# Six of the eight weight-chunk splits moved from setup to beside the first pair product

## The reference, cut to what matters

```python
def cell(h, x):
    gi = x @ W_ih + b_ih
    gh = h @ W_hh + b_hh
    i_r, i_z, i_n = jnp.split(gi, 3, axis=-1)
    h_r, h_z, h_n = jnp.split(gh, 3, axis=-1)
    r = jax.nn.sigmoid(i_r + h_r)
    z = jax.nn.sigmoid(i_z + h_z)
    n = jnp.tanh(i_n + r * h_n)
    h_new = (1.0 - z) * n + z * h
    return (h_new, h_new)
...
x = x + ffn(gru(cond_2048, x))
```

## Time and profile before

| | us |
|---|---|
| median of the runs | 2902.66 |
| the profiled execution's own time | 2908.95 |
| its span, first to last instruction | 2907.2 |
| setup, to the start of the next block | 139.26 |
| PE busy in the span | 2569.9 (88%) |
| DVE busy | 1682.8 (58%) |
| POOL busy | 1240.1 (43%) |
| ACT busy | 1141.0 (39%) |

### The profile page before, as it was taken

One profiled execution on the slowest core, in us unless ns is written; L12 is line 12 of the kernel. 1 busy time (PEld: TensorE's weight loads), 2 busy tenths in 40 slices (PEclk: granted clock), 3 DMA queues, 4 the chain that ended last, 5 costly groups with the idle time before them and its releaser, 6 DMA issues. The chain is left out here.

```text
span 2907.2 us, 154632 instructions
## 1 busy us (share of the span) xinstructions
PE 2569.9 (88%) x67605; PEld 1678.1 (58%) x67605; DVE 1682.8 (58%) x3398; ACT 1141.0 (39%) x2317; POOL 1240.1 (43%) x598
## 2 busy tenths in 40 slices
PE   2088999999889999998999999999996999999995
PEld 1066777776768888886664564745542444444442
DVE  8852222226622222226628778877483888888886
ACT  1312222225622222225603333323233777777773
POOL 0255666662156666662160450704501333333333
PEclk8599999999999999999999999999997999999997
DMA  6833222224422222226463352443522232322321
GB/s 192 237 84 79 73 70 73 73 73 116 129 62 72 71 73 71 71 73 174 135 155 113 99 161 85 137 147 95 165 93 91 66 93 80 94 83 86 91 57 51
DMA packets 234843, 293.74 MB, mean 101 GB/s; under 512 B 69581, under 2 KB 194023, under 8 KB 233895
## 3 DMA queue, kind: packets, MB, share of 16 engines
q1 hardware_dynamic: 212743, 240.84, 29.6%
q10 hardware_dynamic: 18304, 36.19, 3.6%
q0 software_dynamic: 3680, 15.21, 1.8%
HBM read 231.61 MB, written 60.45 MB: 100 GB/s over the span
## 5 line engine op out<-in xcount | busy, mean ns | idle before, releaser
L1145 PE MATMUL psum<-second_shared 64*32 64x384 f16 x32768 | 1026.9, 324 | 52.3 <-issue 33.8
L1153 PE MATMUL psum<-low_w,low_hot 64*32 64x384 f16 x16384 | 758.7, 324 | 3.2 <-issue 3.2
L1372 DVE TENSOR_SCALAR second_shared<-psum 32x384 f16<-32x384 f32 x496 | 272.3, 549 | 747.7 <-PE psum L1145 740.4
L953 POOL TENSOR_TENSOR low_hot<-first_shared,sum_mask 128x1024 f16<-128x1024 f16 x256 | 500.4, 1955 | 468.8 <-DVE first_shared L1359 196.1
L1145 PEld LDWEIGHTS psum<-second_shared 64*32 64x32 f16 x32768 | 562.7, 93 | 201.5 <-issue 94.6
L947 POOL TENSOR_TENSOR second_shared<-first_shared,whole_mask 128x2048 f16<-128x2048 f16 x128 | 462.7, 3615 | 456.1 <-PE psum L1145 346.0
L1044 ACT ACTIVATE second_shared<-psum 32x384 f16<-32x384 f32 x496 | 239.8, 483 | 800.3 <-PE psum L1145 794.4
L1233 PE MATMUL psum<-low_w,low_hot 64*64 64x384 f16 x12288 | 515.5, 326 | 16.8 <-issue 11.1
L1233 PEld LDWEIGHTS psum<-low_w,low_hot 64*64 64x64 f16 x12288 | 374.6, 108 | 152.8 <-issue 17.2
L310 PE MATMUL psum<-w_x,x_cols 128*64 128x512 f32 (+1 forms) x1856 | 310.8, 493 | 9.4 <-ACT x_cols L280 9.4
L1153 PEld LDWEIGHTS psum<-low_w,low_hot 64*32 64x32 f16 x16384 | 283.7, 93 | 57.9 <-issue 5.0
(11 more groups left out here) (286 smaller groups left out, 2722.7 us busy)
## 6 DMA issues: line engine op xcount, KB each, us to landing
low_w<-w_rows SPq DMA_DIRECT2D x384, 144.0 KB
low_w<-w_rows SPq DMA_DIRECT2D x256, 120.0 KB
second_shared<-w_rows SPq DMA_DIRECT2D x1024, 24.0 KB, 1.8
x_gates<-x_out ACTq DMA_DIRECT2D x58, 384.0 KB, 2.3
xg<-x_gates SPq DMA_DIRECT2D x58, 384.0 KB, 3.2
low_w<-w_rows SPq DMA_DIRECT2D x256, 72.0 KB
low_w<-w_rows SPq DMA_DIRECT2D x384, 48.0 KB
w_rows<-quantised SPq DMA_DIRECT2D x24, 384.0 KB, 4.7
```

Source lines behind the costliest of these rows:

```text
L953: nc.gpsimd.tensor_tensor(low_hot[:, buf].rearrange("p (s k) b -> p s k b", s=SUBS), low_a[:, slot, bass.ds(c, 1), :, :].rearrange("p a s ...
L1145: last = nc.tensor.matmul(run[m][u][j * Q:(j + 1) * Q, :], whole_hot[rows[u], m, sign, kk, j % 2 * Q:(j % 2 + 1) * Q], whole_w[rows[u], m, ...
L1153: nc.tensor.matmul(run[m][u][j * Q:(j + 1) * Q, :], low_hot[rows[u], m, kk, j % 2 * Q:(j % 2 + 1) * Q], low_w[rows[u], m, at:at + UC], sta ...
L1372: last = nc.vector.tensor_scalar(whole_w[u * B:u * B + Q, m, 0, bq, :], run[m][u][bq * Q:(bq + 1) * Q, :], 1.0 / HIGH_ONE, None, ALU.mult)
```

## The change

Setup now splits jobs 0 and 1 (chunk 0 of W_ih and chunk 0 of W_hh). Jobs 2 to 7 are the other six chunks in the order of use. They are loaded again from DRAM by ACT's queue (load_more), scaled by ACT, split by DVE and written by SP and POOL within the pair product of step 0. DVE gets three split operations behind the copies of a block: a "slot" is the place behind the copies for block b = slot + 2, and job j has slots 3(j-1), 3(j-1)+1 and 3(j-1)+2, so jobs 2 to 7 fill slots 3 to 20. The 33 operations of cut_later follow three by three from slot 22. In SP's queue write_first_kinds(job) stands behind the load of block 3(j-1)+3; in POOL's, write_second_kinds(job) stands behind the operands of that same block; ACT makes the W3 copy behind its copies in the job's third slot, and scales the next job two slots ahead of its first one. The first 24 rounds (48 blocks) of SP, POOL and ACT are straight code. Setup's read-back of the state's pieces moves to SP's queue, and both read-backs come ahead of the second chunk's last copies. The semaphore split_link counts seven of a job's nine operations (not the sixth and the ninth, which raise rest_ok and split_ok).

```diff
+            CHUNKS = 2 * KD
+            CHUNK_ORDER = [m * KD + k for k in range(KD) for m in range(2)]
+            FIRST_CHUNKS = 2
+            SPLIT_LINKS = 7
+            SPLIT_OPS = 9
...
+            def cut_done(job, link):
+
+                return SPLIT_LINKS * job + 1 + link
+
+            def write_first_kinds(sp, job):
+
+                for kind, link in ((W0, 1), (W1, 3), (W2, 5)):
+                    sp.wait_ge(split_link, cut_done(job, link))
+                    write_kind(sp, job, kind, moved)
+
+            def write_second_kinds(pool, job):
+
+                pool.wait_ge(split_link, cut_done(job, 6))
+                write_kind(pool, job, W00, moved_second)
+                pool.wait_ge(w3_ok, job + 1)
+                write_kind(pool, job, W3, moved_second)
+                pool.wait_ge(split_ok, job + 1)
+                write_kind(pool, job, WX, moved_second)
...
+            def copy_w3(a, job, left):
+
+                a.wait_ge(rest_ok, job + 1)
+                nc.scalar.activation(split[:, job % 2, W3, :], left, ACT.Copy).then_inc(w3_ok, 1)
...
+            def split_chunk(v, job, left):
+
+                mine = split[:, job % 2]
+                n = [SPLIT_LINKS * job]
+
+                def link(ins):
+                    n[0] += 1
+                    ins.then_inc(split_link, 1)
+                    v.wait_ge(split_link, n[0])
+
+                v.wait_ge(scaled, 2 * (job + 1))
+                if job >= 2:
+                    for done in (moved, moved_second):
+                        v.wait_ge(done[job % 2], 16 * 3 * (job // 2))
+                yield link(nc.vector.tensor_scalar(mine[:, W0, :], left, GRID_ONE, GRID_ONE, ALU.add, ALU.subtract))
+                yield link(nc.vector.tensor_tensor(left, left, mine[:, W0, :], ALU.subtract))
+                yield link(nc.vector.tensor_scalar(mine[:, W1, :], left, GRID_DOWN, GRID_DOWN, ALU.add, ALU.subtract))
+                yield link(nc.vector.tensor_tensor(left, left, mine[:, W1, :], ALU.subtract))
+                yield link(nc.vector.tensor_copy(mine[:, W2, :], left))
+                yield nc.vector.tensor_tensor(left, left, mine[:, W2, :], ALU.subtract).then_inc(rest_ok, 1)
+                yield link(nc.vector.tensor_scalar(mine[:, W00, :], mine[:, W0, :], GRID_UP, GRID_UP, ALU.add, ALU.subtract))
+                yield link(nc.vector.tensor_tensor(mine[:, WX, :], mine[:, W0, :], mine[:, W00, :], ALU.subtract))
+                yield nc.vector.tensor_tensor(mine[:, WX, :], mine[:, WX, :], mine[:, W1, :], ALU.add).then_inc(split_ok, 1)
...
-                        for n in range(CHUNKS):
-                            if n < 2:
-                                sp.wait_ge(first_cut, CUTS * (n + 1))
-                                put_pieces(sp, (0, H0)[n], first_split[:, n])
-                            for kind, link in ((W0, 1), (W1, 3), (W2, 5)):
-                                sp.wait_ge(pk, cut_done(n, link))
-                                write_kind(sp, n, kind, moved)
+                        for n in range(2):
+                            sp.wait_ge(first_cut, CUTS * (n + 1))
+                            put_pieces(sp, (0, H0)[n], first_split[:, n])
+                        write_first_kinds(sp, 0)
+                        sp.wait_ge(pieces_out, 2 * PIECES_OUT)
+                        load_low(sp, H0, LOW_ROWS, ROWS_H)
+                        write_first_kinds(sp, 1)
+                        load_whole(sp, H0, 1, ROWS_H)
...
+                        for job in range(FIRST_CHUNKS):
+                            write_second_kinds(pool, job)
...
+                        a.wait_ge(id_ok, 1)
+                        for m in range(2):
+                            for part in range(2):
+                                own = slice(part * B, part * B + Q)
+                                for bq in range(2):
+                                    nc.scalar.activation(whole_a[own, m, :, bq * Q:(bq + 1) * Q], ident[own, own].unsqueeze(1).to_broadcast([Q, NBK, Q]),
+                                                         ACT.Copy, scale=HIGH_ONE)
...
+                        for job in range(FIRST_CHUNKS):
+                            a.wait_ge(raw_in[CHUNK_ORDER[job]], 16)
+                            scale_chunk(job, raw[:, CHUNK_ORDER[job], :], rest[:, job, :])
+                        a.wait_ge(pieces_out, 2 * PIECES_OUT)
+                        load_low(a, 0, LOW_ROWS, ROWS_X0)
+                        copy_w3(a, 0, rest[:, 0, :])
+                        load_whole(a, 0, 0, ROWS_X0)
+                        copy_w3(a, 1, rest[:, 1, :])
...
+                        for c in range(FIRST_CHUNKS):
+                            for _ in split_chunk(v, c, rest[:, c, :]):
+                                pass
...
+                later_split = [gates_x[:, n, :].bitcast(F16).rearrange("p (a c) -> p a c", a=A_KINDS) for n in range(len(LATER))]
+                later_rest = [gates_h[:, n * KD * B:(n + 1) * KD * B] for n in range(2)]
+                more_raw = [spare[:, n * G3:(n + 1) * G3] for n in range(2)]
+                more_rest = [spare[:, (2 + n) * G3:(3 + n) * G3] for n in range(2)]
+                MORE = range(FIRST_CHUNKS, CHUNKS)
+                JOB_SLOTS = SPLIT_OPS // 3
+                LATER_FROM = JOB_SLOTS * (len(MORE) + 1) + 1
+                UNROLLED = 24
+
+                PIECES_AT = (18, 20, 22)
+
+                def job_slot(job):
+
+                    return JOB_SLOTS * (job - FIRST_CHUNKS + 1)
+
+                def job_at(slot):
+
+                    return next((job for job in MORE if job_slot(job) == slot), None)
...
-                        for c in range(2):
+                        for c in range(UNROLLED):
                             for m in range(2):
+                                if c >= PB and c % PB == 0:
+                                    for done in (moved, moved_second):
+                                        sp.wait_ge(done[m], 16 * 3 * (c // PB + 1))
                                 load(0, m, c, m)
-                        for n, t in enumerate(LATER):
-                            sp.wait_ge(later_cut, CUTS * (n + 1))
-                            put_pieces(sp, t, later_split[n])
-                            for m in range(2):
-                                load(0, m, 2 + n, m)
+                                job = job_at(2 * c + m - JOB_SLOTS)
+                                if job is not None:
+                                    write_first_kinds(sp, job)
+                            if c in PIECES_AT:
+                                n = PIECES_AT.index(c)
+                                sp.wait_ge(later_cut, CUTS * (n + 1))
+                                put_pieces(sp, LATER[n], later_split[n])
                         sp.wait_ge(pieces_out, PIECES_OUT * (2 + len(LATER)))
                         load_low(sp, 2, SUM_ROWS, ROWS_X2)
-                        pair_blocks(sp, pair_load(0), 2 + len(LATER))
+                        for m in range(2):
+                            for done in (moved, moved_second):
+                                sp.wait_ge(done[m], 16 * 3 * KD)
+                        pair_blocks(sp, pair_load(0), UNROLLED)
...
-                            for c in range(FIRST if t else 0):
+                            first = FIRST if t else UNROLLED
+                            for c in range(first):
                                 for m in range(2):
                                     both(c, m)
-                            pair_blocks(pool, both, FIRST if t else 0)
+                                    job = job_at(2 * c + m - JOB_SLOTS)
+                                    if t == 0 and job is not None:
+                                        write_second_kinds(pool, job)
...
-                            load_rows(a, j)
-
                         def x_window(t):
...
+                            if t > 0:
+                                pair_blocks(a, base, 1)
+                                return
+                            for c in range(1, UNROLLED):
+                                for m in range(2):
+                                    base(c, m)
+                                    slot = 2 * (c - 1) + m
+                                    job = job_at(slot - 2)
+                                    if job is not None:
+                                        copy_w3(a, job, more_rest[job % 2])
+                                    job = job_at(slot + JOB_SLOTS - 1)
+                                    if job is not None:
+                                        more_scaled(job)
+                            pair_blocks(a, base, UNROLLED)
+
+                        def load_more(job):
+
+                            n = CHUNK_ORDER[job]
+                            a.dma_start(more_raw[job % 2], w_src[n // KD][n % KD * P:(n % KD + 1) * P, :]).then_inc(more_in[job % 2], 16)
+
+                        def more_scaled(job):
+
```

(74 more changed lines are left out.)

70 lines of the change are left out of this document (4 added, 66 removed).

## The result

The changed kernel takes 2913.9 us (median of 6 runs, 2910.6 to 2917.8), the kernel before, on the same chip, 2903.2 (2902.3 to 2905.3): ratio 1.0034, 95% interval 1.0022 to 1.0046. It is 10.7 us slower. The forecast was 2895, 7 us faster: the sign was wrong. Executions that ran at a far lower granted clock (two of e8's six, at 0.74 and 0.38) are left out of every number.

A forecast was written before the change was run, and what follows sets the result against it. DVE was taken to set the pace in setup, and PE, at 8.2 us a block, in the pair product. Setup -59.0, pair product +50.1 and reload +1.6 gave -7.3 us: 2895 us, range 2883 to 2907.

The forecast's parts named there:

- The step that failed: Job's third slot, pair product: SP's loads, issued behind its W2 write, land at 30.0 us, just ahead of POOL's masks.
- The masks: Pair product: POOL's masks for block s+4 wait behind its writes, ending at 31.1 instead of 24.6: 6.5 us stall per job.
- the exclusion: Pair product: DVE's split operations and POOL's instructions wait for each other; without it, stalls of 3.2 us, 19 in all.
- E+7.3: Forecast end of a job's operation 9, 7.3 us after E, where its third slot begins and ACT's copies start.
- the term for ACT's reload: Pair product: 768 KB reloads meet late loads, +0.3 us four times and 0.5 at the start, together +1.6 us.
- rival 3: Pair product: the split's traffic makes loads late in every slot, twelve slots losing 2.3 us each; +19, 2922 us; chance 0.18.
- Setup: Weight splitting before the product: splitting fewer chunks ends it at 80.2 us, with ACT's chain last: -59.0 us.
- The start: Beginning of the pair product: reload for jobs 2 and 3 delays it by 0.5 us.
- Behind load_low: The 7.38 us idle time behind load_low moves to about block 48 and stays unchanged.
- The clock: Pair product: PE's clock falls behind each of six stalls, costing 2.25 us more each: 13.5 us.
- the rivals: Four alternative outcomes for the whole kernel: 2872 us (chance 0.18), 2846 (0.04), 2922 (0.18) and 2904 (0.10).

The follow-up runs named there:

- e8: Changed kernel with SP's and POOL's writes one block later, W2 and W00 released one operation earlier, and the reload of chunks 2 and 3 behind ACT's first copy: 2880.0 us.
- e10: Changed kernel with POOL's eighteen writes in the product on 128 of 1536 columns and the loads reading the first block's rows: 2887.3 us, ratio 0.9955.
- e3: Changed kernel with only POOL's writes of a job moved one block later in its queue, SP's left in place: 2924.6 us, ratio 1.0072.
- e4: Changed kernel with W0, W1, W2 and W00 waiting for operations 1, 3, 5 and 7 in place of 2, 4, 7 and 8: 2892.8 us, ratio 0.9964.
- e2: Changed kernel with only SP's writes of a job moved one block later in its queue, POOL's left in place: 2890.0 us, ratio 0.9952.
- e6: Changed kernel without jobs 2 to 7, all loads of weight rows reading the first block's rows: 2844.8 us, ratio 0.9815.
- e1: Changed kernel with both SP's and POOL's writes of a job moved one block later in their queues: 2868.7 us, ratio 0.9886.
- e5: Changed kernel with the nine DVE operations of jobs 2 to 7 on 8 of 1536 columns: 2891.4 us, ratio 0.9975.
- e7: Changed kernel with SP's and POOL's writes one block later and DVE's split operations of jobs 2 to 7 on 8 of 1536 columns: 2882.8 us, ratio 0.9933.
- e9: Changed kernel with SP's writes one block later and POOL's three writes spread over three successive blocks, the first one block later: 2865.0 us, ratio 0.9883.
- e11: As e9, plus WX ahead of W3, ACT's W3 copy one slot later, and the reload of chunks 2 and 3 behind ACT's first copy: 2868.0 us, ratio 0.9887.

## Why the prediction was wrong

**The step that failed** is "SP: W2 issued at 22.6, loads to 28.2, landed at 30.0, just ahead of POOL." The load's issue was counted at 5.6 us. The trace has 8.6, then 2.4 to landing instead of 1.8. The load, not the masks, was last, and the stall was 8.1 instead of 6.5 in the typical case. e10 shows the cause, what POOL's writes have in flight; e3 shows the switch inside one load; e4 and e2, which move the load away from those writes, make POOL's masks last as forecast. This step decides the sign: e10, where the load is issued at the forecast's pace, is 13 us faster than before (1 - 0.9955).

**The masks** were put at 6.5 us. e2 measures 3.8 to 5.6. The mechanism, the exclusion, was right: in the product L282 takes 3.9 us on average against 1.76 in setup, while L1453, which reads PSUM, keeps its 0.55:

```profile
L1453 DVE TENSOR_SCALAR second_shared<-psum 32x384 f16<-32x384 f32 x88 | 48.3, 549 | 82.4 <-PE psum L1227 80.9
L282 DVE TENSOR_TENSOR ex_tmp<-ex_tmp,quantised 128x1536 f32<-128x1536 f32 x6 | 23.4, 3901 | 0.2
```

The Trainium skill says the same in kind (GPSIMD Engine Reference, the table of specifications: SBUF interfaces shared with VectorE, with contention for instructions in a two-port mode or with two SBUF inputs).

But operation 9 ended at E+6.2 (263.15 against 256.97), not E+7.3, so the masks came 1.4 us earlier than forecast. Operation 7 was done earlier too, which hid part of the load's error: from the forecast's own W2 at E+6.2, 8.6 us of issue and 2.4 to landing would end at E+17.2, where 16.0 was measured.

**Blocks 6 and 12** had only 0.3 us each, in the term for ACT's reload. Their loads are issued at the normal 1.75 us for four, but land some 5 us after issue, and ACT's reload of 768 KB and two of SP's writes go out within 3 us of the last issue: 2.4 and 2.7 us of stall. That these two are the cause is read from the timeline, not tested. That is rival 3's mechanism, in two blocks rather than in all twelve.

**The rest.** Setup: -57.2 for -59.0, and ACT's chain last, as forecast; in part by luck, as ACT's copy came 3.2 us later than counted and the end of setup 1.4 us sooner behind it. The start: +3.1 where 0.5 was taken; e6 and e8 show that the reload of 1.5 MB ahead of the product makes it (3.8 and 3.9 us of idle time less). Behind load_low: +2.3 where nothing was taken; e1 has 7.73, the changed kernel and e2 9.7, so it differs between kernels that do the same there, and its cause is open. The three smaller waits, 2.2 us, had no term. The clock: seven falls to 0.50 to 0.69 for 4.6 us, (1 - clock) x 4.6 summed, 12.0 us for the 13.5 of the forecast. The sum then is 48.4 of stalls + 2.3 + 2.2 + 12.0 - 2.1 fewer pauses for issue = 62.8 of the 63.8 us; 1.0 has no name.

**Of the rivals** none was right as a whole. Rival 3's price, +19, was nearest to +10.7, for half of its reason: DMAs slowed by the split's traffic. I had dismissed it since most writes go out while SP is waiting. The writes that mattered are POOL's, and they start when SP is no longer waiting, because operations 7 and 8, which release the load and POOL's writes, are 1 us apart.

The Trainium skill (DMA: Bandwidth & Descriptors, "Issuing engines are not separate DMA queues") states that DMAs from all issuing engines run on the same 16 engines and interleave. The runs agree with it, and they show that not only the transfer but also the issue is held: with POOL's whole writes in flight SP's load takes 8.6 us to issue, with a twelfth of their bytes 5.8.

## What to carry to other kernels

Work moved beside a loop must not stand in the loop's own queues ahead of its loads: place each write behind the load it might hold, one block later, even if its data is ready sooner. Here that placement alone, without one instruction less, was worth 43 us (1.0034 - 0.9886), more than the whole of what the change lost or won. When several queues are released by neighbouring links of one chain, their DMAs start together: count the issue time of a load at what it is under that traffic.

## What the hardware did that I had not expected

- A DMA's issue time depends on what other queues have in flight. Four DMAs of 24 KB take 1.75 us. Where POOL's three writes go out together shortly ahead of it or within it, with SP's W2 or all three of SP's writes near them (1.5 to 2.4 MB), one row of four takes 3.2 to 4.9 (the changed kernel, e1, e2, e3, e5, e7). With POOL's share cut to a twelfth it takes at most 1.94 (e10), with POOL's writes one block apart at most 2.54 (e9).
- PE's clock behind short stalls is not a matter of their length alone. I took it over the 4.6 us behind every idle time of 2.30 us and more in the pair products of the thirteen traces (0.50 is the 1.2 GHz level, what lies between is a mean over both). Behind all 65 of 3.67 us and more it read 0.50 to 0.71. Of the 23 between 2.30 and 3.66 it stayed at 1.00 behind twelve (2.87, 3.11, 3.28 and 3.56 among them) and fell behind eleven (2.30, 2.47, 2.68 and 3.66 among them). At that length a stall costs its own time alone or 1.3 to 2.3 us more, which is as much as the differences between e1, e7, e9 and e11.
